# Experts and final norm of a decoder layer as one unrolled stage: pairs in the first two thirds of the shared products, norms of two batches beside the rest

## What is computed

```python
logits = x @ router_weight.T                       # 64 experts, 6 per token
hmid = gelu(einsum('ech,ehf->ecf', xs, w1))        # xs: up to 96 gathered tokens per expert
y = einsum('ecf,efh->ech', hmid, w2)
out = zeros.at[token_of].add(y_pair)               # y times the gate, summed per token
shared = gelu(x @ sw1.T) @ sw2.T                   # shared expert, width 512, all tokens
x = layernorm(x + out + shared)
```

## Time and profile before

| | us |
|---|---|
| median of 3 runs (2213.58 to 2217.93) | 2215.46 |
| the profiled execution, all of it | 2225.81 |
| its span, first to last instruction | 2224.0 |
| experts stage: first load issued, first transposes, last add issued | 1795.2, 1802.9, 2120.2 |
| norm stage: first load issued, end | 2130.4, 2224.0 |

### The profile page before, as it was taken

The page is one execution under the profiler, slowest core; times in us unless marked ns, Lnnn a source line. Parts: engine busy times, 40 slices in busy tenths (PEclk is TensorE's granted clock), DMA queues, the critical chain, the costliest instruction groups (busy, mean ns, idle before and its releaser), DMA issues. The chain is left out here.

```text
span 2224.0 us, 46491 instructions
## 1 busy us (share of the span) xinstructions
PE 1711.4 (77%) x14688; PEld 1214.7 (55%) x14688; DVE 1303.0 (59%) x3032; ACT 1075.7 (48%) x1670; POOL 1236.8 (56%) x1287
## 2 busy tenths in 40 slices
PE   1489999999999845888888888888886359999900
PEld 1356666666666523555555555555553248888800
DVE  2366767676676624777777777777776212222258
ACT  0266666666666523666666666656655112222200
POOL 1566767676676311166666666666665725555423
PEclk9699999999999976988999999989989579999955
DMA  5566666767677426654554545555550035555445
GB/s 197 125 138 158 153 163 147 171 149 171 158 153 168 100 72 106 124 109 98 106 102 101 101 101 102 99 96 103 99 87 25 14 99 124 129 127 126 96 128 179
DMA packets 288971, 267.15 MB, mean 120 GB/s; under 512 B 78962, under 2 KB 273364, under 8 KB 278640
## 3 DMA queue, kind: packets, MB, share of 16 engines
q1 hardware_dynamic: 257648, 244.57, 48.6%
q0 software_dynamic: 22528, 13.03, 3.9%
q10 hardware_dynamic: 8704, 8.39, 1.1%
HBM read 170.57 MB, written 94.30 MB: 119 GB/s over the span
## 5 line engine op out<-in xcount | busy, mean ns | idle before, releaser
L1592 POOL DMA_INDIRECT slot_table<-cross_tok_i,cross_slot_i x384 | 382.6, 996 | 144.6 <-issue 109.3
L598 DVE TENSOR_REDUCE self_nmax<-self_p_mx 128x2 f32<-128x512 f32 x512 | 329.4, 687 | 214.2 <-PE self_p_mx L340 213.8
L1423 DVE TENSOR_REDUCE cross_nmax<-cross_p_mx 128x8 f32<-128x960 f32 x256 | 295.0, 1152 | 210.8 <-PE cross_p_mx L1053 160.0
L510 ACT ACTIVATE self_probs<-self_p_sc 128x1024 f32<-128x1024 f32 x256 | 261.3, 1021 | 95.2 <-PE self_p_sc L328 93.0
L1279 ACT ACTIVATE cross_probs<-cross_p_sc 120x1024 f32<-120x1024 f32 x256 | 261.3, 1021 | 86.0 <-PE cross_p_sc L1037 55.4
L340 PE MATMUL self_p_mx<-self_k_stack,self_q_stack 96*128 96x256 bf16 x1024 | 160.5, 278 | 64.5 <-DMA self_k_stack<-self_k_parts 61.3
L1069 PE MATMUL cross_p_pv<-cross_probs,cross_v_aug 120*32 120x256 f32 x2048 | 176.8, 418 | 9.9 <-ACT cross_probs L1279 6.1
L1053 PE MATMUL cross_p_mx<-cross_k_stack,cross_q_stack 48*128 48x120 bf16 x2048 | 104.5, 225 | 100.4 <-DVE cross_nmax L1423 63.5
L328 PE MATMUL self_p_sc<-self_q_stack,self_k_stack 99*128 99x256 bf16 x1024 | 157.3, 276 | 13.3 <-ACT self_probs L510 12.8
L1956 POOL DMA_INDIRECT expert_sums<-ffn_ye,ffn_idx_add x64 | 92.5, 1445 | 122.0 <-DMA expert_sums<-ffn_ye,ffn_idx_add 53.4
L1037 PE MATMUL cross_p_sc<-cross_q_stack,cross_k_stack 51*128 51x256 bf16 x1024 | 105.8, 287 | 56.5 <-ACT cross_probs L1279 46.7
(11 more groups left out here) (180 smaller groups left out, 3767.6 us busy)
## 6 DMA issues: line engine op xcount, KB each, us to landing
self_q_stack<-self_q_parts SPq DMA_DIRECT2D x64, 256.0 KB, 5.9
cross_q_stack<-cross_q_parts SPq DMA_DIRECT2D x128, 128.0 KB
ffn_w<-in_ffn_w SPq DMA_DIRECT2D x64, 256.0 KB
self_q_parts<-self_parts SPq DMA_DIRECT2D x32, 384.0 KB, 2.8
self_k_parts<-self_parts SPq DMA_DIRECT2D x32, 384.0 KB, 3.8
self_k_stack<-self_k_parts SPq DMA_DIRECT2D x32, 384.0 KB, 8.0
cross_q_parts<-cross_parts SPq DMA_DIRECT2D x64, 192.0 KB
expert_sums<-zero_rows SPq DMA_DIRECT2D x8, 1024.0 KB, 10.2
```

The source lines that it names most:

```text
L510: act.activation(probs[:, g % 4, :], p_sc[:, :, :].rearrange("p b n -> p (b n)"), ACT.Exp, scale=SCALE).then_inc(s_exp, 1)
L598: dve.tensor_reduce(nmax[:, M.slot, :, m], p_mx[:, m % 2, :].rearrange("p (c k) -> p c k", c=TC), AX_X, ALU.max, negate=True).then_inc(s_r ...
L1423: dve.tensor_reduce(nmax[:, M.slot, :, :, 2 * m:2 * m + 2].rearrange("p c e h -> p e h c"), p_mx[:, :, 0:4 * KEYS].rearrange("p e (x k) -> ...
L1592: pool.indirect_dma_start(out=route[:, :], out_offset=bass.IndirectOffsetOnAxis(ap=slot_i[:, Q.slot, tc, k:k + 1], axis=0), in_=tok_i[:, Q ...
```

## The change

`experts`, `finish`, `run_steps` and `Batch` go; `feed_forward` takes their place, as one block whose steps are all written out, with constants in place of registers. A step u is half a batch: even ones have the transposes of x and the second shared product, odd ones the first shared product. Pair k has its gather at step 9k/8 (rounded down), so there is a pair in 8 of 9 steps up to step 34; its transposes, hidden layer, output and adds come 2, 3, 4 and 5 steps later. Gather buffers and expert weights are four deep, x and ye three, xT and xgT two; the slots column is the index itself, without a copy. The norm of two batches (f = 0 to 15) stands at steps 43, 44, 46, 47, 49, 50 and so on to 64, 65: sums loaded two steps before (after the last add), sum and statistics on VectorE, four operations on GpSimd, the scaling one step later on ScalarE (Identity with scale and bias) ahead of that step's gelus, the store two steps later on SyncE's queue.

```diff
...
-def experts(nc, outer, n_batches, W, C, x2, table, moe, acc):
+def feed_forward(nc, outer, n_batches, W, C, x2, table, moe, out):
...
+    EJ = 2
+    N_PAIRS = N_EXP // EJ
     ROW = DM + N_EXP
+    SK = SHARED // P
+    NF = n_batches // 2
+    FT = 2 * TC
+    NX = 4
+    GATHER = [k * 9 // 8 for k in range(N_PAIRS)]
+    LAST_Y = 2 * n_batches
+    FINISH = [LAST_Y + 1 - (NF - 1 - f) * 3 // 2 for f in range(NF)]
+    END = LAST_Y + 5
+    gather_at = {u: k for k, u in enumerate(GATHER)}
+    turn_at = {u + 2: k for k, u in enumerate(GATHER)}
+    hidden_at = {u + 3: k for k, u in enumerate(GATHER)}
+    out_at = {u + 4: k for k, u in enumerate(GATHER)}
+    add_at = {u + 5: k for k, u in enumerate(GATHER)}
+    weights_at = {u - 1: k for k, u in enumerate(GATHER)}
+    rows_at = {u - 2: f for f, u in enumerate(FINISH)}
+    finish_at = {u: f for f, u in enumerate(FINISH)}
+    scale_at = {u + 1: f for f, u in enumerate(FINISH)}
+    store_at = {u + 2: f for f, u in enumerate(FINISH)}
...
...
+        xg = sb("xg", [CAP, NX, EJ, ROW])
+        xT = sb("xT", [P, 2, FC, T])
+        ye = sb("ye", [CAP, 3, EJ, DM])
+        m_sb = sb("m_sb", [P, 3, FT, DM])
...
+            for u in range(-4, END):
+                if u % 2 == 0 and 0 <= u // 2 + 2 < n_batches:
+                    t = u // 2 + 2
+                    if t >= 3:
+                        sp.wait_ge(s_y, t - 2)
+                    sp.dma_start(x_sb[:, t % 3, :, :], x_rows[t][:, :, 0:DM]).then_inc(s_x[t % 3], 16)
+                if u in weights_at:
+                    k = weights_at[u]
+                    if k >= NX:
+                        sp.wait_ge(s_hep, k - NX + 1)
+                        sp.wait_ge(s_yep, k - NX + 1)
...
+                if u in rows_at:
+                    f = rows_at[u]
+                    sp.wait_ge(s_add, 16 * N_EXP)
+                    if f >= 3:
+                        sp.wait_ge(s_sum, f - 2)
+                    sp.dma_start(m_sb[:, f % 3, :, :], m_rows[f]).then_inc(s_m[f % 3], 16)
+                if u in store_at:
+                    f = store_at[u]
+                    sp.wait_ge(s_o, f + 1)
+                    sp.dma_start(o_rows[f], o_sb[:, f % 2, :, :]).then_inc(s_out[f % 2], 16)
+            for p in range(2):
+                sp.wait_ge(s_out[p], 16 * (NF // 2))
...
+            for u in range(END):
+                t, second = u // 2, u % 2
+                if u in turn_at:
+                    k = turn_at[u]
+                    pe.wait_ge(s_g[k % NX], 16 * EJ * (k // NX + 1))
+                    if k:
+                        pe.wait_ge(s_gT, k)
...
+                    mm.then_inc(s_gp, 1)
+                if not second and t < n_batches:
+                    pe.wait_ge(s_x[t % 3], 16 * (t // 3 + 1))
+                    if t:
+                        pe.wait_ge(s_xT, t)
...
                     mm.then_inc(s_xp, 1)
+                if u in hidden_at:
+                    k = hidden_at[u]
+                    pe.wait_ge(s_gT, k + 1)
+                    pe.wait_ge(s_we[k % NX], 32 * (k // NX + 1))
+                    if k:
+                        pe.wait_ge(s_he, k)
...
+                    mm.then_inc(s_hep, 1)
+                if not second and 1 <= t <= n_batches:
+                    b = t - 1
+                    pe.wait_ge(s_h, 2 * (b + 1))
+                    if b:
+                        pe.wait_ge(s_y, b)
...
                     mm.then_inc(s_yp, 1)
+                if second and t < n_batches:
+                    pe.wait_ge(s_xT, t + 1)
+                    for k in range(SK):
+                        if k % 2 == 0 and t:
+                            pe.wait_ge(s_h, 2 * (t - 1) + k // 2 + 1)
...
+                        if k % 2 == 1:
+                            mm.then_inc(s_hp, 1)
+                if u in out_at:
+                    k = out_at[u]
+                    pe.wait_ge(s_he, k + 1)
+                    if k:
+                        pe.wait_ge(s_ye, k)
...
                     mm.then_inc(s_yep, 1)
...
         @block.scalar
         def _(act):
+            for u in range(END):
+                t, second = u // 2, u % 2
+                if not second and t < n_batches:
+                    act.wait_ge(s_xp, t + 1)
+                    if t >= 2:
+                        act.wait_ge(s_hp, 2 * (t - 1))
+                    act.activation(xT[:, t % 2, :, :].rearrange("p f n -> p (f n)"), p_x[:, :], ACT.Copy)\
+                       .then_inc(s_xT, 1)
+                if u in hidden_at:
+                    k = hidden_at[u]
+                    act.wait_ge(s_hep, k + 1)
...
+                if u in scale_at:
+                    f = scale_at[u]
+                    act.wait_ge(s_sh, f + 1)
+                    if f >= 2:
+                        act.wait_ge(s_out[f % 2], 16 * (f // 2))
+                    for c in range(FT):
+                        ins = act.activation(o_sb[:, f % 2, c, :], r_sb[:, f % 2, c, :], ACT.Identity,
+                                             bias=shift[:, f % 2, c:c + 1], scale=rstd[:, f % 2, c:c + 1])
+                    ins.then_inc(s_o, 1)
+                if second and t < n_batches:
                     for k in range(2):
+                        act.wait_ge(s_hp, 2 * t + k + 1)
+                        if t >= 2:
+                            act.wait_ge(s_yp, t - 1)
+                        act.activation(hT[:, t % 2, 2 * k:2 * k + 2, :].rearrange("p k n -> p (k n)"), p_h[:, k, :],
                                        ACT.Gelu_apprx_tanh).then_inc(s_h, 1)
         @block.vector
         def _(dve):
             dve.memset(xg[:, :, :, :], 0.0).then_inc(s_z, 1)
+            dve.memset(neg_half[:, :], -0.5).then_inc(s_z, 1)
+            for u in range(END):
+                t, second = u // 2, u % 2
+                if u in turn_at:
+                    k = turn_at[u]
+                    dve.wait_ge(s_gp, k + 1)
...
+                if not second and 1 <= t <= n_batches:
+                    b = t - 1
+                    dve.wait_ge(s_yp, b + 1)
+                    dve.tensor_tensor(acc[:, b * TC * DM:(b + 1) * TC * DM], p_y[:, :],
+                                      x_sb[:, b % 3, :, :].rearrange("p c n -> p (c n)"), ALU.add).then_inc(s_y, 1)
+                if u in out_at:
+                    k = out_at[u]
+                    dve.wait_ge(s_wc, k + 1)
+                    dve.wait_ge(s_yep, k + 1)
+                    if k >= 3:
+                        dve.wait_ge(s_add, 16 * EJ * (k - 2))
                     for j in range(EJ):
+                        ins = dve.tensor_scalar(ye[:, k % 3, j, :], p_ye[0:CAP, j * DM:(j + 1) * DM],
+                                                wcol[:, k % NX, j:j + 1], None, ALU.mult)
                     ins.then_inc(s_ye, 1)
+                if u in finish_at:
+                    f = finish_at[u]
+                    dve.wait_ge(s_m[f % 3], 16 * (f // 3 + 1))
+                    dve.wait_ge(s_y, 2 * (f + 1))
+                    if f >= 2:
+                        dve.wait_ge(s_o, f - 1)
+                    dve.tensor_tensor(r_sb[:, f % 2, :, :].rearrange("p c n -> p (c n)"),
+                                      m_sb[:, f % 3, :, :].rearrange("p c n -> p (c n)"),
+                                      acc[:, f * FT * DM:(f + 1) * FT * DM], ALU.add).then_inc(s_sum, 1)
+                    dve.wait_ge(s_sum, f + 1)
+                    if f:
+                        dve.wait_ge(s_mv, f)
+                    for c in range(FT):
+                        ins = dve.bn_stats(stats[:, c, :], r_sb[:, f % 2, c, :])
+                    ins.then_inc(s_st, 1)
+                    dve.wait_ge(s_st, f + 1)
+                    if f >= 2:
+                        dve.wait_ge(s_sh, f - 1)
+                    for c in range(FT):
+                        ins = dve.bn_aggr(mv[:, f % 2, c, :], stats[:, c, :])
+                    ins.then_inc(s_mv, 1)
...
+            def gather(k, j):
+                e = k * EJ + j
...
+            def add(k, j):
+                e = k * EJ + j
+                if e:
+                    pool.wait_ge(s_add, 16 * e)
+                pool.indirect_dma_start(
...
+            for u in range(END):
+                if u in gather_at:
+                    k = gather_at[u]
+                    if k >= NX:
+                        pool.wait_ge(s_gp, k - NX + 1)
...
+                    gather(k, 0)
+                if u in add_at:
+                    pool.wait_ge(s_ye, add_at[u] + 1)
+                    add(add_at[u], 0)
+                if u in gather_at:
+                    gather(gather_at[u], 1)
+                if u in add_at:
+                    add(add_at[u], 1)
+                if u in finish_at:
+                    f = finish_at[u]
+                    pool.wait_ge(s_mv, f + 1)
+                    if f >= 1:
+                        pool.wait_ge(s_sh, f)
...
```

(47 more changed lines are left out.)

274 lines of the change are left out of this document (51 added, 223 removed).

## The result

| | us |
|---|---|
| before, median of 4 runs (2213.58 to 2217.93) | 2215.69 |
| changed, median of 4 runs (2258.61 to 2269.65) | 2263.92 |
| changed, the profiled execution and its span | 2262.31, 2260.5 |

The ratio is 1.0217, 95% interval 1.0197 to 1.0237: slower by 48 us, where 31 were forecast. The medians are the better measure. So I count the stage from its first load on SyncE's queue to the end of the span: 428.8 us before (from 1795.18), 477.9 now (from 1782.63), which is +49.1 and agrees with the medians. A second profile of the changed kernel, on another chip, gives 477.5.

The account below looks back on a forecast made before the run. TensorE bounds the experts loop, serial adds nearly so, then VectorE the norms. Part 1 gains 23 us, part 2 takes 147 against 94; execution 2257.0, +31.2 on the median 2215.5 gives 2246.7 us, range 2212 to 2266.

Parts of the forecast that it names:

- Y(22): Sixteen TensorE matmuls into p_y (second shared product) for batch 22, first after the last add; forecast to start at 2124.4.
- Y(22) to Y(31): Last ten second shared products: six steps of 12.8 us, three of 7.7, plus 10.2 for six cold restarts.
- The distance between adds: GpSimd's serial adds into expert_sums, each waiting for the one before: 4.4 us apart, bounds 4.18 and 4.66.
- part 1: Expert pairs at 8 in 9 half steps: the serial adds set the pace; gains 23 us in all.
- The cold restart: TensorE at clock 0.50 after idling: 1.7 us lost on each next Y, bounds nothing and 2.0.
- part 2: Norms beside remaining shared products: ScalarE's scale ahead of the gelus holds TensorE; 147 us where the norm stage took 94.
- long steps: Y to Y with a norm at an even step, add, norm, GpSimd, scale and gelus in one chain: 12.8 us.
- Edits with one answer: Index copies, constants, buffers, Identity beside gelu and unrolling: no cost or gain; table-load bound 16 us more.
- (2): Rival, chance 0.15: norms run beside the products, Y follows Y in 7.7 us; 51 us under the forecast, at 2196.
- (3): Rival near 2216, chance 0.09: adds at 4.18 (-14 us) and no slow restarts (-12), or norm chain partly hidden.
- (4): Rival on GpSimd: adds behind queued gathers are late, 31 x 1.8 = +56 us; chance 0.06 together with (5).
- (5): Rival: TensorE's clock stays at 0.50 in part 1, up to +83 us; chance 0.06 together with (4).

Follow-up runs that it names:

- The run with that order: Changed kernel with ScalarE's scaling of the norm rows moved behind the two gelus of the same step: 1.0029 of the kernel before.
- two tables: Changed kernel with a second DRAM table of sums for odd experts and ScalarE's scale after the gelus: 0.9725 of the kernel before, 2170.09 us.

## Why the prediction came out as it did

Right in sign, in the mechanism of both parts and inside its range of 2212 to 2266, but close to its upper end: 2263.92 us was measured, 17 more than 2246.7, because two terms were set too small. Stage by stage, counted from the first load:

| step of the sum | forecast | measured | difference |
|---|---|---|---|
| first load to first add | 31.1 | 31.5 | +0.4 |
| 63 distances between adds | 277.2 | 290.6 | +13.4 |
| last add landed, loads issued | 4.3 | 3.4 | -0.9 |
| load of sums to norm 0 | 4.0 | 3.9 | -0.1 |
| norm 0 to Y(22) | 12.6 | 11.8 | -0.8 |
| Y(22) to Y(31) | 110.1 | 115.8 | +5.7 |
| tail from Y(31) | 20.8 | 20.8 | 0 |
| stage | 460.0 | 477.9 | +17.9 |

**The distance between adds** (part 1) is the term that was mis-sized: 4.4 forecast, 4.61 measured, and 4.66 was the bound. 4.4 was taken from the late adds of the earlier trace rows. Earlier in that stage TensorE set the pace, so their distances could not be read as a limit, and I took the last stretch for the whole. Without the expert loads the distance is 4.36; they are half or more of what a mean over the stage had to include. Nor were the adds "without holes": 17 distances are over 4.8. That the last add starts at 2104.78, as forecast (2104), is luck: this execution entered the stage 12.6 us earlier, and the adds took 13.4 us longer.

**The cold restart** (part 2) was set at 1.7 us from the earlier trace rows, a restart after 1.96 us idle. After the 5 to 6 us of this chain, and after 9.91 us for the first, the seven cold Y took 5.16, 6.23, 6.70, 5.33, 6.24, 6.78 and 5.29 us, on average 2.3 over 3.62, above the bound of 2.0. The six before Y(31) cost 14.7 in place of 10.2: 4.5 of the 5.7 us. The run with matmuls in the waits shows that this is the restart and not something beside it. The clock in these Y was between the two levels, not at 0.50 throughout as forecast: over the seven it was 0.71, 0.59, 0.55, 0.69, 0.59, 0.54 and 0.69, and the lower it was, the longer they took. The forecast took its loss from one stretch of 3.30 us; the groups here lost 1.5 to 3.2 us each over 3.62.

**Within the chain two errors cancel in part.** A norm takes VectorE 3.2 us (2129.67 to 2132.83) where 3.4 stood, so that was too much. GpSimd takes 2.0 us (2156.66 to 2158.62) in three of the six long steps and 2.8 (2132.83 to 2135.67) in the other three, where 1.85 stood; its power operation alone is 1.04 us. A long step with a warm Y is therefore 12.6 us (2149.13 to 2161.71) in three cases and 13.4 in three, as the run with 11 and 22 added matmuls shows (2145.60 to 2158.97), against 12.8. The short ones are 7.9 against 7.7. Together this is the 1.2 us that remain of the 5.7.

**Edits with one answer.** Identity beside gelu brought no further table load: the stage has one, of 1.28 us, as before. The Trainium skill, "ScalarE: Activation LUTs", section on table sets, had said so, and the trace agrees. Unrolling gained nothing: where nothing waits, TensorE is busy 191.16 of 192.00 us in unrolled code (two tables) and was 281.87 of 282.00 in the loop.

**The rivals.** (2), that the norms run beside the products, needed the other order. The run with that order shows that its price was wrong too: a stage of 439.3 us where (2) had 409. Of these 30 us the adds are 16.6 (4.66 apiece), Y(22) to Y(31) 8.0 (77.3 against 69.3), the way from last add to Y(22) 3.9. (3) would have needed 4.18 and no restarts; both went the other way. (4): with the same gathers in the queue and no expert loads the mean distance is 4.36, so a gather ahead of an add doesn't make it 1.8 us late. (5): the clock was 0.90 in part 1, and TensorE still waited 53.3 us for gathers, so it didn't matter.

## What to carry to other kernels

Before work is laid beside other work, read each engine's queue in order: a wait for a slow chain, placed ahead of the short operation that the bounding engine needs, costs the whole chain at each step; here two blocks exchanged were worth 1.9%. A serial chain of DMAs, each waiting for the one before to land, is a bound of its own. Packing the work beside it more tightly only makes it the pace, and it pays to break the dependence (a second table) before rearranging. A term that occurs 63 times deserves its size from a stretch with the traffic that it will meet, not from the quietest.

## What the runs showed of the hardware

An operation of GpSimd on 128x4 elements takes 0.23 us alone, and 1.11 and 1.17 us when VectorE's sum of two 128x1024 operands runs beside it: those at 2065.63 and 2066.82 above each end about when VectorE's sum does, and the one at 2069.85, with no sum beside it, takes 0.23. The Trainium skill, "SBUF — State Buffer", section "Who interferes with whom", says that a VectorE instruction with two SBUF inputs and a GpSimd instruction that reads SBUF exclude one another, one blocking until the other is done; the trace agrees, and each costs 0.9 us in the norm chain. In the changed kernel this is what makes GpSimd's part 2.8 us instead of 2.0 in three of the six long steps.

A cold restart did not have one price: groups of the same sixteen matmuls took 5.2 to 6.8 us after idle times of 5.0 to 9.9 us, with no order by the length of the idle time (5.16 us after 9.91, 6.70 after 4.97). It goes with the granted clock over the group: 0.71 in the one of 5.16 us, 0.54 in the one of 6.78, where 0.50 is the 1.2 GHz level and 1.00 the 2.4 GHz level. Before Y(22), from 2117.00 to 2123.80 with TensorE idle, it was 0.50; in the H behind each of the first two cold Y it was 1.00.
